# Loads of wk issued by ScalarE's queue, wq moved up on SyncE's, six warm-up matmuls in place of nine

## The reference

```
q = (layernorm(x) @ Wq) * SCALE
k = (context @ Wk) * SCALE
v = context @ Wv
attn = softmax(q k^T)
x = x + (attn v) @ Wo + bo
x = x + ffn(layernorm(x))      # square(relu(x Ws1)) Ws2, and experts whose weight trunc(softmax) is nonzero
```

## Time and profile before

| | |
|---|---|
| median of 3 runs | 118.31 us (118.0, 118.31, 119.46) |
| profiled execution | 118.02 us |
| its span, first to last instruction | 116.2 us |
| TensorE busy | 109.9 us, 95% |
| VectorE, ScalarE, GpSimd busy | 90.1, 84.6, 63.4 us |
| DMA | 12.70 MB |

### The profile page before, as it was taken

The page is one execution under the profiler, slowest core; times in us unless marked ns, Lnnn a source line. Parts: engine busy times, 40 slices in busy tenths (PEclk is TensorE's granted clock), DMA queues, the critical chain, the costliest instruction groups (busy, mean ns, idle before and its releaser), DMA issues.

```text
span 116.2 us, 3116 instructions
## 1 busy us (share of the span) xinstructions
PE 109.9 (95%) x854; PEld 106.1 (91%) x854; DVE 90.1 (77%) x351; ACT 84.6 (73%) x345; POOL 63.4 (55%) x103
## 2 busy tenths in 40 slices
PE   6997999999899989999999999999999999989981
PEld 6986989998798889999999999999999999979970
DVE  0039987996978597887979797887979696798963
ACT  4016544899659879898989899898989789994320
POOL 2000173359616965786676578657746865369250
PEclk9999999999999999999999999999999999999997
DMA  3799999994000100022005000400400050031033
GB/s 65 249 343 351 352 338 351 351 348 159 0 8 0 71 19 0 6 102 78 0 0 181 0 0 36 145 0 0 177 4 0 0 181 6 0 120 60 29 140 102
DMA packets 11815, 12.70 MB, mean 109 GB/s; under 512 B 1056, under 2 KB 10272, under 8 KB 11808
## 3 DMA queue, kind: packets, MB, share of 16 engines
q1 hardware_dynamic: 11520, 12.36, 32.1%
q10 hardware_dynamic: 288, 0.26, 0.7%
HBM read 8.42 MB, written 2.10 MB: 91 GB/s over the span
## 4 chain that ended last, share of the span: by engine, by line
PE 67%; DVE 12%; ACT 10%; DMA 4%; issue 3%; SPq 2%; DVEq 0%; ACTq 0%
ACT probs L695 8%; PE o_ps L420 7%; PE o_ps L422 7%; PE o_ps L421 7%; PE s_ps L420 6%; PE s_ps L422 6%; PE s_ps L421 6%; PE g_ps L479 5%; PE f_ps L509 4%; DMA wqt_sb<-in_wq_t 4%; PE s_ps L414 3%; PE g_ps L492 2%; PE f_ps L420 2%; DVE row_max L911 2%; DVE u_lo L1032 2%
## 5 line engine op out<-in xcount | busy, mean ns | idle before, releaser
L695 ACT ACTIVATE probs<-s_ps,neg_max,rstd 128x77 f32<-128x77 f32 x128 | 51.5, 424 | 8.8 <-DVE neg_max L919 8.7
L815 POOL TENSOR_TENSOR probs<-probs,recip 128x308 f32<-128x308 f32 x31 | 21.7, 701 | 23.7 <-DVE recip L925 23.7
L695 ACT ACTIVATION_READ_ACCUMULATOR probs<-s_ps,neg_max,rstd 128x1 f32 x128 | 27.3, 213 | 0.0
L420 PE MATMUL o_ps<-u_hi,pt_hi 128*128 128x256 f32 (+1 forms) x80 | 22.7, 284 | 0.9 <-DVE pt_lo L933 0.5
L422 PE MATMUL o_ps<-u_lo,pt_hi 128*128 128x256 f32 (+1 forms) x80 | 22.3, 279 | 0.0
L421 PE MATMUL o_ps<-u_hi,pt_lo 128*128 128x256 f32 (+1 forms) x80 | 22.3, 279 | 0.0
L420 PE MATMUL s_ps<-a_hi,xt_hi 128*128 128x308 f32 x64 | 22.0, 344 | 0.0
L422 PE MATMUL s_ps<-a_lo,xt_hi 128*128 128x308 f32 x64 | 19.5, 304 | 0.0
L421 PE MATMUL s_ps<-a_hi,xt_lo 128*128 128x308 f32 x64 | 19.4, 303 | 0.0
L420 PEld LDWEIGHTS o_ps<-u_hi,pt_hi 128*128 128x128 f32 (+1 forms) x80 | 15.0, 188 | 1.5 <-DVE pt_lo L933 0.9
L421 PEld LDWEIGHTS o_ps<-u_hi,pt_lo 128*128 128x128 f32 (+1 forms) x80 | 15.1, 189 | 0.0
(11 more groups left out here) (163 smaller groups left out, 253.4 us busy)
## 6 DMA issues: line engine op xcount, KB each, us to landing
xt_sb<-in_x_t SPq DMA_DIRECT2D x8, 256.0 KB, 6.4
x_sb<-in_x SPq DMA_DIRECT2D x8, 256.0 KB, 6.5
x_sb<-x_tr SPq DMA_DIRECT2D x7, 256.0 KB, 2.3
out<-y_sb SPq DMA_DIRECT2D x6, 256.0 KB, 2.3
wqt_sb<-in_wq_t SPq DMA_DIRECT2D x4, 256.0 KB, 5.1
wo_sb<-in_wo SPq DMA_DIRECT2D x1, 1024.0 KB, 8.8
wk_sb<-in_wk_p SPq DMA_DIRECT2D x3, 256.0 KB, 3.2
wv_sb<-in_wv_p SPq DMA_DIRECT2D x2, 384.0 KB, 6.1
```

The lines of the kernel that those rows point to most:

```text
L420: pe.matmul(out_ap, hi, rhs_hi, start=first, stop=False)
L695: e = act.activation(probs[:, par, h * TK:(h + 1) * TK], s_ps[:, 2 * par + half, (h - half * H // 2) * TK:(h - half * H // 2 + 1) * TK], A ...
L815: pool.tensor_tensor(rows, rows, recip[:, par, hs].unsqueeze(2).broadcast_to([P, H // 2, TK]), ALU.mult).then_inc(probs_ready, 1)
```

## The change

The two main loads of wk and wk's tail are taken out of SyncE's program and put at the head of ScalarE's, before its first wait. On SyncE's queue the second context chunk then follows the first, and wq comes straight behind it. TensorE issues six warm-up matmuls in place of nine. Semaphores and all else stay.

```diff
-    WARM_UP = 9
+    WARM_UP = 6
...
             sp.dma_start(ctx_sb[:, 0, :], ctx_p[:, 0, :]).then_inc(ctx_in, 16)
-            for i in range(2):
-                sp.dma_start(wk_sb[:, i, 0:HG, :].rearrange("p e c -> p (e c)"), wk_p[:, i, 0:HG * P]).then_inc(wk_in[i], 16)
             sp.dma_start(ctx_sb[:, 1, :], ctx_p[:, 1, :]).then_inc(ctx_tail_in, 16)
-            sp.dma_start(wk_sb[:, :, HG:WB, :].rearrange("p i e c -> p i (e c)"), wk_p[:, :, HG * P:WB * P]).then_inc(wk_tail_in, 16)
             load_wq(0)
             load_wq(1)
             load_wv(0)
...
+            for i in range(2):
+                act.dma_start(wk_sb[:, i, 0:HG, :].rearrange("p e c -> p (e c)"), wk_p[:, i, 0:HG * P]).then_inc(wk_in[i], 16)
+            act.dma_start(wk_sb[:, :, HG:WB, :].rearrange("p i e c -> p i (e c)"), wk_p[:, :, HG * P:WB * P]).then_inc(wk_tail_in, 16)
             for g in range(H // 2):
                 act.wait_ge(kt_ready, g + 1)
```

## The result

The changed kernel takes 117.86 us (median of 10 runs, 117.16 to 118.34); the kernel before, run between them on the same chip, 118.59 (10 runs, 118.0 to 119.46). The ratio is 0.9921, interval 0.9895 to 0.9948, some 0.9 us: less than the 2% at which a change counts as faster, but clearly not nothing.

What follows compares the result with a forecast made beforehand. It took the start as the bound: wq's loads, VectorE's centring, then TensorE. Filled DMA holes take 1.0 us off the profiled 118.02, giving 117.0, put at 117.1 since that run was below the median; range 116.1 to 118.7.

Steps and rivals of the forecast that it cites:

- the forecast case: Whole kernel: filled DMA holes bring the scores 1.0 us earlier; 117.1 us, own range 116.4 to 117.7, chance 0.53.
- That the start carries through: From the first exponentials at 20.88 us on: whatever the start gains reaches the end whole, uneaten by later loads.
- SyncE: Its issue queue: three issues go, so wq's first pair is issued at about 1.65 us instead of 3.29.
- The stream: DMA traffic from 2 to 6 us: filled holes give 1.0 us, bounds 0 and 1.3.
- the first rival: DMA holes stay, wq's third pair still lands at 10.74, copies of K slightly late: 118.0 to 118.3 us, chance 0.20.
- VectorE's half of the argument: VectorE's centring of wq: chain 1.0 us earlier, third centring at 9.8 us instead of 10.79.
- K: wk's tail lands at 6.9 us, about as before; copies of K start near 7.8, inside 1.1 us of slack.
- the upper bound of 8.8: Latest landing of wk's tail in us, if wk's 768 KiB share the DMA engines equally with SyncE's loads.
- the dry rival: TensorE idles after its warm-up matmuls and does K at the lower clock: 119.5 us or 2.4 more, chance 0.17.
- a sign of being wrong: In the trace: K copies after 9.3 us were listed among the signs that the prediction was wrong.
- ScalarE: Its start: 1.6 us of added issues fit its 6.2 us wait; table load behind them ends at 3.6, costing nothing.
- The warm-up: TensorE's start: six matmuls end at 3.9 us, K's main part at 6.9 instead of 7.3; nothing saved or lost.

## Why the prediction was right, and where it was not

**The time.** The forecast took 1.0 us off; the runs took off 0.9 (0.79% of 118.59). The range, and the view that this lies within what 2% can tell, held. But the 1.0 was taken off one execution, 118.02, at the low end of before's runs; off the median of ten it gives 117.6, so 0.5 of the 0.8 by which the forecast missed is its base. And 117.86 lies outside the forecast case's own 116.4 to 117.7, between that case and the one in which the stream gives nothing (118.0 to 118.3). The wide range held both, so that it held says little of the mechanism.

**That the start carries through** was right, and more exactly than it was put: 100.3 to 100.5 us from the scores to the end in every profile. No later load ate of it.

**SyncE** was right: wq is issued at 1.64 (forecast 1.65).

**The stream** was the term of the sum that was mis-sized. It took 1.0 us, which at 348 GB/s is 350 KB of holes filled; 193 KB were, worth 0.55 us. The shares in the earlier trace rows could have told: against 0.98 the three windows lack 0.13, 0.24 and 0.30, worth 0.7 us as an estimate (0.67/0.98), and only that much of the 1.3 us can be idle engines. In the rest they were busy at a lower rate, as at 150 GB/s with a share of 0.95. I expected both holes between 4 and 6 to go; one stayed, and it belongs to wk's tail: where the tail goes, it goes (150 GB/s at 4 to 5 with the tail back on SyncE), and in two loads it is nearly gone (295 to 337). "wk's tail may be slow by itself" stood under the first rival and was right in this much. wq's first pair came better than forecast (5.78 for 6.6), its third worse (10.55 for 9.75) in the first profile of the kernel after; in its second, of the run again, VectorE's third centring is at 9.83, against 9.8 as forecast. VectorE's half of the argument so holds in some executions.

**K** is the step that failed: "I take 6.9, about as before ... far inside the slack of 1.1 us". The tail landed at 8.45, 7.88 and 9.02, around the upper bound of 8.8 that the text had worked out from equal turns, and K's tails started on either side of 8.5, the point that it had named for the dry rival. That bound was the better guess: wk, which had been ahead of wq, now takes turns with it and with wv (0.76 and 0.70 MB up to 7.0). The copies of K began at 9.38, 8.81 and 9.95, past the 9.3 that the prediction had named as a sign of being wrong in two of three. The slack itself was also counted against the old chain: 1.1 us was what K could lose with VectorE where it was. With VectorE 1.0 earlier, as the same text forecast, the copies had to begin by 8.3, 0.1 behind the 8.24 of before. K's slack was used up and TensorE became the bound, behind the tail by a fixed 9.2 us. In the first profile the two chains are close: by VectorE, as an estimate, the scores could have come at 17.49 (10.58 + 17.70 - 10.79), by TensorE they came at 17.65. In the second it is 16.74 (9.83 + 6.91) against 17.08.

So the sum came out near the forecast by luck, by a way that it did not describe: not VectorE's chain one microsecond shorter with K out of sight, but one chain put in place of another. With the three landings of the tail and its 9.2 the scores are at 17.65 on average; the two unchanged profiles of before say 17.70, those with GpSimd held back or the tail in two loads 18.44 and 18.11. The profiles are too few to give the 0.9 us by themselves; how it divides between a shorter chain and an earlier landing stays open.

The Trainium skill's page "DMA: Bandwidth & Descriptors", section "Issuing engines are not separate DMA queues", says that transfers of different issuing engines interleave on the same 16 DMA engines. The trace agrees: between 5 and 6 us ScalarE's queue moves 0.15 MB and SyncE's 0.06. What the page allows is the sequencer time saved, and the prediction read that as nothing; here it is wq's issue at 1.64 instead of 3.29, more than the whole forecast of 1.0. The rate between 4 and 5 us rose from 195 to 333 GB/s, but the rows do not part what the earlier issue did from what the second queue did.

**ScalarE** was right: the table load went behind the issues, at 2.31, and ended at 3.6. **The warm-up** was right in the time: 1.0026 for six alone, 0.992 with nine kept. Its end of K's main part, 6.9, was not: in the second profile and with the tail as two loads it came at 7.57 and 7.65, since the matmuls stayed near 462 ns to about 6 us. **The dry rival** did not happen: TensorE stood 0.30 us behind the warm-up, and its clock rose all the same at about 5.2, as the lengths of K's matmuls say (ns: min, median, max):

```profile
L388 PE MATMUL s_ps<-ctx_sb,wk_sb x2: 462/528/595, 4.3 to 4.7; 128*128 128x154 f32 x2
...
L388 PE MATMUL s_ps<-ctx_sb,wk_sb x2: 293/294/294, 5.6 to 5.7; 128*128 128x154 f32 x2
```

It was real all the same, as the kernel with the tail first shows.

Not settled: whether the second queue is needed, or only wq ahead of the tail. The change does both at once, and no kernel here puts wq ahead of wk's tail on SyncE's queue alone. Nor whether the tail is slow by its pattern (two pieces of 1 KB for each partition, apart from each other) or by being one load where two could go side by side; splitting changes both. How much of its delay is the turns and how much the tail itself is open too: ahead of wq on SyncE's queue it is in at 7.1, behind wk's main loads on ScalarE's at 7.55 to 8.05 in two loads and at 7.88 to 9.02 in one. And why the landings scatter as they do.

## What to carry to other kernels

When a load is moved to a second queue, ask for each queue which of its loads is now last, and give that one the price of equal turns with the other queue before calling its slack enough. Count the slack against the other chain as it will be after the change, not as it was. A low rate is not yet a hole that can be filled: look at the busy share beside it. Work out both chains to the point where they meet, since the one that was covered becomes the bound with no margin left. And where landings scatter by half a microsecond, read the mechanism from several profiles and the size from the medians of runs.

## What the runs showed of the hardware

- The same load of the same kernel lands at different times in different executions: wk's tail at 7.88 and 8.45 (the kernel after twice). With the same loads and another part of the kernel changed it landed at 9.02 (nine warm-up matmuls) and 8.68 (GpSimd waits); wq's first pair, loads as before, landed between 7.62 and 8.45.
- One load of 256 KB in two separate pieces for each partition, on ScalarE's queue, leaves the stream at 155 to 209 GB/s between 5 and 6 us (four profiles); two loads of 128 KB with the same bytes, at 295 to 337 (three). On SyncE's queue alone the difference is not clear: 441 and 396 KB between 4 and 6 us as one load, 480 as two.
- A DMA busy share near 1 does not mean a high rate: 0.95 went with 150 GB/s, 0.98 with 348.
- VectorE's subtraction on 128x512 fp32 takes 0.69 us alone and 1.15 to 1.17 when GpSimd's 0.73 us subtraction has just begun. When VectorE's has begun first (14.01, before), it keeps its 0.69 and GpSimd's cast at 14.07 takes 0.89 instead of 0.40.
- With gaps of 1.46 and 1.09 us in TensorE's early work the granted clock fell to 0.50 at about 8.1 us. With gaps of 0.30 and 1.50 (after), and of 2.23 (after, GpSimd waits), the column stayed at 1.00 and K's tails at their 1.32 us.
